# Two passes by halves in turn, six matmuls of zeros left out, and another order of sixteen chunks in a two-layer attention kernel

## The chip, the core and the metric

The kernel runs on one core of a Trainium2 chip. The metric is the device time in microseconds (us) of one execution. Engines are called as the profile calls them: PE (matmuls), PEld (PE's weight loads), ACT (activations), DVE (vector work), POOL, and SP, which here only issues DMAs; SPq, ACTq and POOLq are the queues of DMA issues.

## The reference, cut to what matters

```python
x = L0_attn_x                                   # (4, 1024, 128), 16 heads of 8
x = _layernorm(x + _L0_attn_ref(x, ...))        # q, k l2-normed over all 128 columns, softmax over 1024 keys
x = _layernorm(x + _L0_ffn_ref(x, ...))         # int8 quantized matmul
x = _layernorm(x + _L1_attn_ref(x, ...))        # layernorm and rope on q, k; causal softmax
x = _layernorm(x + _L1_ffn_ref(x, ...))         # silu(gate) * up, down; 384 hidden
```

Within an attention, for each batch, head and query:

```python
attn = softmax(q @ k.T * scale)                 # layer 1: keys up to the query alone
out = attn @ v
```

## The kernel before

**Chunks, passes, steps.** The 4 x 1024 rows are eight chunks of 512 rows, two to a batch. A layer's attention of one chunk is four *passes* of four heads each. A chunk is written (layer, number): (0, 2) is layer 0's attention for the queries of chunk 2, and needs the keys of chunks 2 and 3; (1, 3) needs the keys of chunks 2 and 3 too, and (1, 2) those of chunk 2 alone, since layer 1 is causal. `CHUNKS` (L48) is the order in which the sixteen pairs are worked through. `pair_steps` (L58) cuts two passes into *steps* of 128 keys by 512 queries for four heads (layer 1 packs parts of steps together). There are 400 steps: 32 in each chunk of layer 0, 10 or 26 in a chunk of layer 1. Step s has the score products k = 2s and 2s+1, two heads each.

**The three engines of a step.** PE makes the scores (`scores`, L964) in one of three slots of PSUM, ACT takes the exponential of each (L820, 800 in all), and PE multiplies the result with v (`sums`, L988). PE runs ahead of ACT: in *slot* s of its program it issues the scores 2s+3 and 2s+4, then the sums of step s-1, then at most one piece of *side work*. The scores of product k wait for exponential k-3. In layer 1 POOL sets the future part of the diagonal blocks to zero before the sums (L728).

**Side work.** All else is cut into pieces that a planner (`side_order`, L174) lays into the slots, by costs and due times: `prep` of a chunk (q, k, v of layer 0), `mid` (end of layer 0's block, its feed-forward part, and q, k, v of layer 1), `last` (end of layer 1's block and its feed-forward part). A job's pieces stay in order; a `mid` is due four slots ahead of the first slot of its chunk. The last two pieces of a `prep` or `mid` are called qkT: PE transposes k (k=1 in the code) and then q (k=0) of the chunk into PSUM, and DVE reads each into `part` as two summands (L1401, L1402). For the planner the qkT of `mid` 7 stand in slots 362 and 363; the first scores of (1, 7), which are product 748, stand in slot 372.

**The way of q and k.** From `part` SP stores them to DRAM, every row four times (`send_parts`, L548: two DMAs for k and two for q), and loads them back as the 128 rows that a pass needs, into `k_st` and `q_st` (`load_rows`, L572: one DMA each). Before a load SP waits until the stores of all chunks that the pass needs have landed, and until the pass four earlier has its scores. SP works through its DMAs in the order of the list `todo` (L634). The first scores of a pass wait for its rows (L969).

**The start.** `prep` of chunks 0 and 1 runs ahead of step 0. So as not to wait for DRAM, pass 0 gets its rows for chunk 0's keys straight from `part` by eight small DMAs (`first_rows`, half on SP, half on ACT), and those for chunk 1's keys by four more (L619), once chunk 1's k is transposed in slot 0; these keys are pass 0's steps 4 to 7. Pass 1's rows come from DRAM as all others do. Products of a tile of zeros (`warm`, `keep_warm`, L1032) stand in places of PE's program where it has nothing else to do, among them three in slot 0 and three in slot 1 (L1074).

Of the kernel before, what the change touches and what calls it, by code (L numbers as in the profile page):

```python
# [15 lines left out]
P = 128  # L16
# [28 lines left out]

CHUNKS = [(0, 0), (0, 1), (0, 2), (0, 3), (1, 0), (0, 4), (1, 1), (0, 5),  # L48
          (1, 2), (0, 6), (1, 3), (0, 7), (1, 4), (1, 5), (1, 6), (1, 7)]
PASSES = [(layer, c // NH2, c % NH2, g) for layer, c in CHUNKS for g in range(GB)]  # L50
NP = len(PASSES)

# [5 lines left out]
def pair_steps(p):  # L58

    layer, b, qh, g = PASSES[p]
    a, z = p, p + 1
    if not layer:
        kts = [[(x, kt)] for x in (a, z) for kt in range(KT)]
    elif qh:
        one = lambda x: [[(x, 0)], [(x, 1)], [(x, 5), (x, 7)], [(x, 2)], [(x, 4)], [(x, 3)]]
        kts = one(a) + [[(a, 6), (z, 6)]] + one(z)  # L70
    else:
        one = lambda x: [[(x, 0)], [(x, 1), (x, 3)]]
        kts = one(a) + [[(a, 2), (z, 2)]] + one(z)
    out = []
    for group in kts:
        tiles, at = [], 0
        for x, kt in group:
            lo = max(kt * P - qh * HALF, 0) if layer else 0
            tiles.append((x, kt, lo, at, HALF - lo))
            at += HALF - lo  # L80
        out.append((tuple(tiles), at, layer == 1 and group[0][1] * P >= qh * HALF))
    return out
# [305 lines left out]
def program(nc, a, ctx):  # L388
# [94 lines left out]
    x_first_in, x_rest_in, head_copied = sem("x_first_in"), sem("x_rest_in"), sem("head_copied")  # L483
    pool_consts, flags_made, late_consts = sem("pool_consts"), sem("flags_made"), sem("late_consts")
    rows_in = [sem(f"rows_in{n}") for n in range(KB)]
    more_rows_in = sem("more_rows_in")
    v_in, more_v_in = sem("v_in"), sem("more_v_in")
    scores_ready = sem("scores_ready")
    probs_ready = sem("probs_ready")
# [27 lines left out]
    shift_out, shift_in = sem("shift_out"), sem("shift_in")  # L517

    POOL_CONSTS = 11
    WARM = (10, 4, 0, 22, 3)  # L520
    NLATE = 9
    layer_job = ("prep", "mid")
    buffers = lambda name, c: job["mid" if (name, c) == ("prep", 1) else name]
# [9 lines left out]

        return b * NH2 + (NH2 if layer == 0 else qh + 1)

    def first_rows(eng, u, dst, y):

        part = job["prep"]["part"][0:P // PRODUCTS, u, y % PARTS if u else y // PARTS, :]
        eng.dma_start(dst[y:P:PRODUCTS, 0, 0:HALF].bitcast(F32), part.bitcast(F32)).then_inc(rows_in[0], 16)

    def parts_sent(eng, name, u, n):

        pools = (name, u) == ("prep", 1) and n > 1
        eng.wait_ge(parts_out[name][u], 16 * PARTS * (n - pools))
        if pools:
            eng.wait_ge(second_k_out, 16 * PARTS)
# [15 lines left out]
    def _(sp):  # L562
# [9 lines left out]
        def load_rows(p):  # L572
            layer, b, qh, g = PASSES[p]
            for u in range(2):
                parts_sent(sp, layer_job[layer], u, 1 if p == 1 and u == 0 else chunks_needed(layer, b, qh))
            if p >= KB:

                sp.wait_ge(scores_ready, 2 * (LAST_STEP[p - KB] + 1))
            keys = keys_of(layer, qh)
            rows(p, 1, k_st[:, p % KB, 0:keys], slice(0, keys), rows_in[p % KB])  # L580
            rows(p, 0, q_st[:, p % KB, :], slice(qh * HALF, (qh + 1) * HALF), rows_in[p % KB])

        def store_parts(name, c, u):
            send_parts(sp, name, c, u)
# [24 lines left out]
        for u, dst in ((1, k_st), (0, q_st)):  # L609
            sp.wait_ge(parts_ready["prep"], 2 - u)  # L610
            for y in range(PRODUCTS // 2):
                first_rows(sp, u, dst, y)
        store_parts("prep", 0, 1)
        store_parts("prep", 0, 0)
        sp.wait_ge(flags_made, 1)
        far_scores = sp.value_load(far_any[0:1, 0:1], min_val=0, max_val=1)
        sp.wait_ge(parts_ready["prep"], 3)
        for y in range(PRODUCTS):
            sp.dma_start(k_st[y:P:PRODUCTS, 0, HALF:S].bitcast(F32),  # L619
                         job["mid"]["part"][0:P // PRODUCTS, 1, y % PARTS, :].bitcast(F32)).then_inc(more_rows_in, 16)  # L620
        load_rows(1)
        store_parts("prep", 1, 0)

        def shift_rows(p):
# [150 lines left out]
    def _(act):  # L775
# [4 lines left out]
        def head():  # L780
# [25 lines left out]
            for u, dst in ((1, k_st), (0, q_st)):  # L806
                act.wait_ge(parts_ready["prep"], 2 - u)
                for y in range(PRODUCTS // 2, PRODUCTS):
                    first_rows(act, u, dst, y)

        head()

# [44 lines left out]
    def _(pe):  # L857
# [106 lines left out]
        def scores(k, shifted):  # L964

            s, tiles_ = k // 2, STEPS[k // 2][1]
            for p in dict.fromkeys(x[0] for x in tiles_):
                if k % 2 == 0 and FIRST[p] == s:
                    pe.wait_ge(rows_in[p % KB], 32 * (p // KB + 1) + (32 * PRODUCTS - 32 if p % KB == 0 else 0))  # L969
                    if shifted:  # L970
                        shifts(p)
            if k % 2 == 0 and tiles_[0][0:2] == (0, TC):
                pe.wait_ge(more_rows_in, 16 * PRODUCTS)
            if k >= SLOTS:

                pe.wait_ge(probs_ready, k - SLOTS + 1)
# [31 lines left out]
        def shifts(p):  # L1008
# [4 lines left out]
                pe.wait_ge(probs_ready, k)  # L1013
            if p == 0:
                pe.wait_ge(more_rows_in, 16 * PRODUCTS)
                pe.wait_ge(pool_consts, POOL_CONSTS + 1)
            for r in range(NR):
                h, t = divmod(r, TC)
# [38 lines left out]
        def steps(shifted):  # L1057
# [10 lines left out]
            for s in range(NS + 1):  # L1068
                for k in (2 * s + 3, 2 * s + 4):
                    if k < 2 * NS:  # L1070
                        scores(k, shifted)
                    if k % 2 and s in BETWEEN:
                        sums(s - 1)
                if s < 2 and not shifted:  # L1074
                    keep_warm(WARM[4], ACC)
                if s and s not in FRONT and s not in BETWEEN:
                    sums(s - 1)
                for name, c, e, what, k in SIDE_ORDER[s]:
# [14 lines left out]
    def _(dve):  # L1093
# [255 lines left out]
        def read(name, c, what, k):  # L1349
# [35 lines left out]
            elif what == "qkT":  # L1385
# [7 lines left out]
                    dve.wait_ge(more_rows_in, 16 * PRODUCTS)  # L1393
                if k == 1 and (name, c) == ("prep", 2):
                    dve.wait_ge(rows_in[0], 32 * PRODUCTS)
                if name == "prep" and k == 0:
                    ch.link(ts(part[:, 0, 0, :], side, tcol, None, ALU.mult))
                    stt(out=part[:, 0, 1, :], in0=side, scalar=tcol, in1=part[:, 0, 0, :].bitcast(F32), op0=ALU.mult,
# [135 lines left out]
```

## Time and profile before

| | |
|---|---|
| median of three runs | 834.07 us (833.52 to 834.15) |
| the profiled execution | 835.72 us, of it 833.6 us from the first to the last instruction (its span) |
| busy: PE, ACT, DVE, POOL | 804.5, 772.8, 540.5, 169.6 us |
| 800 exponentials on ACT | 749.8 us |
| mean granted TensorE clock | 0.991 of full speed |

The span is what the trace shows; the profiled execution's time is 2.1 us longer than its span. PE's busy time is modelled, so a share of 97% doesn't mean that it computes at its peak.

### The profile page before, as it was taken

The page shows a single profiled execution, that of the slowest core. Times are in us where ns is not written, and L with a number is a line of the kernel's source. Part 1 is how long each engine was busy: PE and PEld are TensorE (multiplying, and loading weights), DVE is VectorE, ACT ScalarE, POOL GpSimd, SP SyncE. Part 2 cuts the span into 40 slices and gives each one's busy share as a digit, 9 for nine tenths or more (in the row PEclk, how much of TensorE's full clock was granted, in tenths as well). Part 3 has the DMA queues.
Part 4 walks back from the last instruction along what each step waited for, and adds up shares of the span by engine and source line. Part 5 has one row for each costly group of instructions (what it writes and reads, how often), then busy time and mean ns, then how long its engine had stood idle before and what let it go on. Part 6 is the DMA issues. An engine that isn't in the chain of part 4 may idle for free.

```text
span 833.6 us, 18913 instructions
## 1 busy us (share of the span) xinstructions
PE 804.5 (97%) x7461; PEld 295.6 (35%) x7463; DVE 540.5 (65%) x1426; ACT 772.8 (93%) x869; POOL 169.6 (20%) x370
## 2 busy tenths in 40 slices
PE   8899999999999999999999999999999999999996
PEld 4223332332332433343333433343333343443444
DVE  4165657777867787877563577766664268786656
ACT  4699999999999999999999999999999999899972
POOL 3110000010000701033100521023300263363220
PEclk9799999999999999999999999999999999999999
DMA  5765412341611731173140331331231231062000
GB/s 163 257 195 190 172 45 103 125 141 52 245 47 49 268 135 43 62 247 99 39 152 27 116 103 50 127 103 39 77 127 52 77 116 51 27 202 90 15 14 15
DMA packets 48316, 88.74 MB, mean 106 GB/s; under 512 B 5088, under 2 KB 14432, under 8 KB 48224
## 3 DMA queue, kind: packets, MB, share of 16 engines
q1 hardware_dynamic: 47456, 85.95, 30.6%
q8 instruction: 61, 1.00, 0.5%
q0 software_dynamic: 288, 1.05, 0.4%
q10 hardware_dynamic: 480, 0.48, 0.2%
q14 instruction: 31, 0.25, 0.1%
HBM read 51.03 MB, written 35.65 MB: 104 GB/s over the span
## 4 chain that ended last, share of the span: by engine, by line
PE 75%; ACT 12%; DVE 7%; issue 3%; SPq 1%; DMA 1%; DVEq 0%; ACTq 0%
PE ps L1003 36%; PE ps L981 21%; ACT probs L820 12%; PE ps L873 9%; PE ps L862 3%; PE ps L958 3%; DVE th L1411 1%; DVE hT L1412 1%; DMA k_st<-mid_part 1%; PE ps L867 1%; PE ps L1034 1%; PE ps L1042 0%; SPq L554 0%; DVE sums_t L1240 0%; DVE mid_part L1401 0%
## 5 line engine op out<-in xcount | busy, mean ns | idle before, releaser
L820 ACT ACTIVATE probs<-ps 128x1024 f32<-128x1024 f32 x800 | 749.8, 1054 | 32.6 <-PE ps L981 23.2
L1003 PE MATMUL ps<-probs,v_st 128*32 128x512 f32 (+3 forms) x3584 | 428.5, 560 | 3.1 <-issue 2.4
L981 PE MATMUL ps<-q_st,k_st 32*128 32x512 f32 (+3 forms) x1792 | 266.2, 461 | 9.0 <-ACT probs L820 5.5
L981 PEld LDWEIGHTS ps<-q_st,k_st 32*128 32x128 f32 x1792 | 120.1, 182 | 290.0 <-ACT probs L820 223.6
L728 POOL TENSOR_SCALAR_AFFINE_SELECT probs<-probs 128x256 f32<-128x256 f32 x256 | 103.8, 428 | 143.3 <-ACT probs L820 141.6
L1003 PEld LDWEIGHTS ps<-probs,v_st 128*32 128x32 f32 x3584 | 78.6, 108 | 110.8 <-issue 74.2
L696 POOL COPY v_st<-v_all 128x256 f32<-128x256 f32 (+1 forms) x65 | 28.8, 452 | 365.7 <-PE ps L1003 357.3
L1240 DVE STREAM_TRANSPOSE sums_t<-ps 128x512 f32<-128x512 f32 x32 | 22.9, 716 | 45.2 <-PE ps L1003 44.6
L1381 DVE COPY mid_qkv<-ps 128x384 f32<-128x384 f32 x32 | 17.8, 558 | 35.9 <-PE ps L873 34.8
L958 PE MATMUL ps<-yTp,w_hid 128*128 128x512 f32 x84 | 30.8, 448 | 4.1 <-DVE gate_sb L1406 2.5
L1381 DVE COPY prep_qkv<-ps 128x384 f32<-128x384 f32 x24 | 13.4, 558 | 31.2 <-PE ps L873 30.5
L873 PE MATMUL ps<-w_cols,yT 128*32 128x384 f32 x256 | 26.7, 489 | 0.0
L1411 DVE SCALAR_TENSOR_TENSOR th<-th,gate_sb 128x512 f32<-128x512 f32 x21 | 14.9, 708 | 16.6 <-PE ps L958 16.2
L1416 DVE TENSOR_TENSOR last_y<-ps,last_y 128x128 f32<-128x128 f32 x24 | 7.0, 291 | 28.8 <-PE ps L873 28.4
L873 PE MATMUL ps<-w_down,hT 128*32 128x128 f32 x672 | 23.8, 275 | 1.1 <-DVE last_y L1416 0.6
L718 POOL TENSOR_TENSOR x_all<-x_all,vecs 128x512 f32<-128x512 f32 x16 | 23.3, 1458 | 0.0
L958 PEld LDWEIGHTS ps<-yTp,w_hid 128*128 128x128 f32 x84 | 12.5, 188 | 29.6 <-issue 9.4
L1358 DVE TENSOR_TENSOR x_all<-ps,x_all 128x512 f32<-128x512 f32 x15 | 10.4, 692 | 19.1 <-PE ps L873 11.5
L873 PEld LDWEIGHTS ps<-w_down,hT 128*32 128x32 f32 x672 | 17.9, 110 | 13.2 <-issue 7.5
L1406 DVE COPY gate_sb<-ps 128x512 f32<-128x512 f32 x21 | 14.5, 691 | 12.3 <-PE ps L958 12.0
L873 PE MATMUL ps<-w_cols,xT 128*32 128x384 f32 x192 | 20.1, 491 | 0.4 <-DVE hT L1412 0.2
L1401 DVE CAST mid_part<-ps 128x512 fp32r<-128x512 f32 x17 | 11.8, 692 | 11.9 <-PE ps L862 11.7
(190 smaller groups left out, 634.7 us busy)
## 6 DMA issues: line engine op xcount, KB each, us to landing
k_st<-parts_scratch SPq DMA_DIRECT2D x47, 512.0 KB, 3.6
parts_scratch<-mid_part SPq DMA_DIRECT2D x34, 512.0 KB, 4.3
q_st<-parts_scratch SPq DMA_DIRECT2D x63, 256.0 KB, 3.9
parts_scratch<-prep_part SPq DMA_DIRECT2D x28, 512.0 KB, 4.7
k_st<-parts_scratch SPq DMA_DIRECT2D x16, 256.0 KB, 2.9
xT<-in_xT SPq DMA_DIRECT2D x8, 256.0 KB, 4.3
x_all<-in_x SPq DMA_DIRECT2D x8, 256.0 KB, 5.5
out<-yo SPq DMA_DIRECT2D x7, 256.0 KB, 2.3
```

The source lines that it names most:

```text
L696: return g_.tensor_copy(v_st[:, p % VB, t, :, p % 2 * SR:p % 2 * SR + D], v_all[:, layer, b % 2, t, g * GH * D:(g + 1) * GH * D] .rearrang ...
L718: g_.tensor_tensor(x_all[:, c, :, :], x_all[:, c, :, :], bc(vecs[:, 3 * layer, :].unsqueeze(1), [P, TC, C]), ALU.add).then_inc(bias_added, 1)
L728: op = g_.affine_select(out=block_, in_=block_, compare_op=ALU.is_ge, fill=0.0, base=0, pattern=[[0, 2], [1, P]], channel_multiplier=-1)
L820: nc.scalar.activation(probs[:, k % PS, :, 0:w], slot(k)[:, :, 0:w], ACT.Exp).then_inc(probs_ready, 1)
L862: last_ = tp(dst[:, t * P:(t + 1) * P], src(t), idn[:])
L873: last_ = mm(dst[row, :], src[:, row], w, start=first, stop=last)
L958: last_ = mm(side, w_hid[:, 0 if what == "gate" else 1, k * P:(k + 1) * P], yTp[:, n, :], start=(n == 0), stop=(n == PARTS - 1))
L981: last_ = mm(slot(k)[:, e, at:at + n], k_st[row, p % KB, kt * P:(kt + 1) * P], q_st[row, p % KB, lo:HALF], start=True, stop=not shifted)
L1003: last_ = mm(acc[HR * h:HR * (h + 1), lo:HALF], v_st[:, p % VB, kt, h, :], probs[:, (2 * s + h // 2) % PS, h % 2, at:at + n], start=FIRST[ ...
L1240: v.transpose(sums_t[:], acc).then_inc(sums_turned, 1)
L1381: v.tensor_copy(job[name]["qkv"][:, k, :], side[:, 0:3 * C]).then_inc(side_read, 1)
L1411: chain[lane(name, c)].link(stt(out=th[:, k % 2, :], in0=th[:, k % 2, :], scalar=1.0, in1=gate_sb[:, k % 2, :], op0=ALU.add, op1=ALU.mult))
```

## The change

Three parts. The order of chunks: every chunk of layer 1 but the last two stands one place sooner; (1, 0) now follows (0, 2), where it followed (0, 3), and so on to (1, 5), which still follows (0, 7), while (1, 4) now stands ahead of (0, 7). The first two passes: their steps go pass 0 with chunk 0's keys, pass 1 with chunk 0's keys, pass 0 with chunk 1's keys, pass 1 with chunk 1's keys. For this pass 1's rows for chunk 0's keys are sent from `part` too, by eight DMAs on SP ahead of all stores, and the stores of chunk 0 stand behind the four DMAs of L619; pass 1's other keys come from DRAM by a load of their own with a semaphore of its own. The products of zeros in slots 0 and 1 are gone.

```diff
-CHUNKS = [(0, 0), (0, 1), (0, 2), (0, 3), (1, 0), (0, 4), (1, 1), (0, 5),
-          (1, 2), (0, 6), (1, 3), (0, 7), (1, 4), (1, 5), (1, 6), (1, 7)]
+CHUNKS = [(0, 0), (0, 1), (0, 2), (1, 0), (0, 3), (1, 1), (0, 4), (1, 2), (0, 5), (1, 3), (0, 6), (1, 4), (0, 7), (1, 5),
+          (1, 6), (1, 7)]
...
         kts = [[(x, kt)] for x in (a, z) for kt in range(KT)]
+        if not p:
+            kts = [[(x, kt)] for n in range(2) for x in (a, z) for kt in range(n * TC, (n + 1) * TC)]
...
-    WARM = (10, 4, 0, 22, 3)
+    WARM = (10, 4, 0, 22)
...
-    def first_rows(eng, u, dst, y):
-
-        part = job["prep"]["part"][0:P // PRODUCTS, u, y % PARTS if u else y // PARTS, :]
-        eng.dma_start(dst[y:P:PRODUCTS, 0, 0:HALF].bitcast(F32), part.bitcast(F32)).then_inc(rows_in[0], 16)
+    def first_rows(eng, p, u, dst, y):
+
+        part = job["prep"]["part"][p * HR:(p + 1) * HR, u, y % PARTS if u else y // PARTS, :]
+        eng.dma_start(dst[y:P:PRODUCTS, p, 0:HALF].bitcast(F32), part.bitcast(F32)).then_inc(rows_in[p], 16)
...
             for y in range(PRODUCTS // 2):
-                first_rows(sp, u, dst, y)
-        store_parts("prep", 0, 1)
-        store_parts("prep", 0, 0)
+                first_rows(sp, 0, u, dst, y)
+        for u, dst in ((1, k_st), (0, q_st)):
+            for y in range(PRODUCTS):
+                first_rows(sp, 1, u, dst, y)
...
-        load_rows(1)
+        store_parts("prep", 0, 1)
+        store_parts("prep", 0, 0)
+        parts_sent(sp, "prep", 1, 2)
+        rows(1, 1, k_st[:, 1, HALF:S], slice(HALF, S), second_rows_in)
         store_parts("prep", 1, 0)
...
-                    pe.wait_ge(rows_in[p % KB], 32 * (p // KB + 1) + (32 * PRODUCTS - 32 if p % KB == 0 else 0))
+                    pe.wait_ge(rows_in[p % KB], 32 * (p // KB + 1) + (32 * PRODUCTS - 32 if p % KB < 2 else 0))
...
+            if k % 2 == 0 and tiles_[0][0:2] == (1, TC):
+                pe.wait_ge(second_rows_in, 16)
...
-                if s < 2 and not shifted:
-                    keep_warm(WARM[4], ACC)
...
                 if k == 1 and (name, c) == ("prep", 2):
                     dve.wait_ge(rows_in[0], 32 * PRODUCTS)
+                    dve.wait_ge(rows_in[1], 32 * PRODUCTS)
```

**PE at the start.** These are PE's rows from the first scores (`ps<-q_st,k_st`) on; `mid_qk` holds chunk 1's k and q there, `warm` the zeros, and `probs,v_st` are sums. Before:

```order
L981 MATMUL ps<-q_st,k_st 128x512 x6
L862 MATMUL ps<-ident,mid_qk 128x128 x4
L981 MATMUL ps<-q_st,k_st 128x512 x4
L1034 MATMUL ps<-warm 128x512 x3
L981 MATMUL ps<-q_st,k_st 128x512 x4
L1034 MATMUL ps<-warm 128x512 x3
L1003 MATMUL ps<-probs,v_st 32x512 x4
L862 MATMUL ps<-ident,mid_qk 128x128 x4
```

Now:

```order
L989 MATMUL ps<-q_st,k_st 128x512 x6
L868 MATMUL ps<-ident,mid_qk 128x128 x4
L989 MATMUL ps<-q_st,k_st 128x512 x8
L1011 MATMUL ps<-probs,v_st 32x512 x4
L868 MATMUL ps<-ident,mid_qk 128x128 x4
```

The two groups of zeros are gone and nothing else moved there; from the ninth score product on the rows are pass 1's, where they were pass 0's second half of keys.

**SP at the start.** These are SP's DMAs from the first rows for pass 0 on (`k_st<-prep_part`) up to the stores of chunk 1's q (`parts_scratch<-mid_part`). Before:

```order
L539 DMA k_st<-prep_part 32x512 x2
L539 DMA q_st<-prep_part 32x512 x2
L554 DMA parts_scratch<-prep_part 256x1x512 x2
L554 DMA parts_scratch<-prep_part 128x2x512 x2
L616 TENSOR_LOAD far_any
L616 ISA x2
L619 DMA k_st<-mid_part 32x512 x4
L570 DMA k_st<-parts_scratch 128x1024
L570 DMA q_st<-parts_scratch 128x512
L554 DMA parts_scratch<-mid_part 128x2x512 x2
```

Now:

```order
L541 DMA k_st<-prep_part 32x512 x2
L541 DMA q_st<-prep_part 32x512 x2
L541 DMA k_st<-prep_part 32x512 x4
L541 DMA q_st<-prep_part 32x512 x4
L619 TENSOR_LOAD far_any
L619 ISA x2
L622 DMA k_st<-mid_part 32x512 x4
L556 DMA parts_scratch<-prep_part 256x1x512 x2
L556 DMA parts_scratch<-prep_part 128x2x512 x2
L572 DMA k_st<-parts_scratch 128x512
L556 DMA parts_scratch<-mid_part 128x2x512 x2
```

Eight small DMAs for pass 1 came in where the four stores of chunk 0 stood; the stores moved behind the four DMAs for chunk 1's keys, and pass 1's load from DRAM is k's second half alone.

**PE in the chunk (1, 6).** These are PE's rows in slots 366 to 369: the projection of the chunk before (`w_out,attn`), scores and sums of (1, 6), and the places where the two qkT of `mid` 7 (`ident,mid_qk`) may stand. Before:

```order
L873 MATMUL ps<-w_out,attn 32x128 x16
L981 MATMUL ps<-q_st,k_st 128x384 x2
L981 MATMUL ps<-q_st,k_st 128x128 x2
L981 MATMUL ps<-q_st,k_st 128x512 x2
L1003 MATMUL ps<-probs,v_st 32x256 x8
L981 MATMUL ps<-q_st,k_st 128x512 x2
L981 MATMUL ps<-q_st,k_st 128x384 x2
L981 MATMUL ps<-q_st,k_st 128x128 x2
L1003 MATMUL ps<-probs,v_st 32x512 x4
L981 MATMUL ps<-q_st,k_st 128x384 x2
```

Now:

```order
L879 MATMUL ps<-w_out,attn 32x128 x16
L989 MATMUL ps<-q_st,k_st 128x384 x2
L989 MATMUL ps<-q_st,k_st 128x128 x2
L989 MATMUL ps<-q_st,k_st 128x512 x2
L1011 MATMUL ps<-probs,v_st 32x256 x8
L868 MATMUL ps<-ident,mid_qk 128x128 x4
L989 MATMUL ps<-q_st,k_st 128x512 x2
L989 MATMUL ps<-q_st,k_st 128x384 x2
L989 MATMUL ps<-q_st,k_st 128x128 x2
L1011 MATMUL ps<-probs,v_st 32x512 x4
L868 MATMUL ps<-ident,mid_qk 128x128 x4
```

The two qkT of `mid` 7 now stand behind the projection, in slots 367 and 368; before they stood in slots 362 and 363, ahead of the first rows shown. The first scores of (1, 7) stand in slot 372 in both.

## Rows read from the trace of the kernel before

**Rows 1.** The page's busy time by engine, and its costliest group.

```profile
PE 804.5 (97%) x7461; PEld 295.6 (35%) x7463; DVE 540.5 (65%) x1426; ACT 772.8 (93%) x869; POOL 169.6 (20%) x370
...
L820 ACT ACTIVATE probs<-ps 128x1024 f32<-128x1024 f32 x800 | 749.8, 1054 | 32.6 <-PE ps L981 23.2
```

**Rows 2.** Timeline of ACT from 18 to 64 us: start, length, [idle before].

```profile
27.57 1.02 ACT L820 ACTIVATE probs<-ps 128x1024 f32<-128x1024 f32 x1 [0.61 <-PE ps L981]
31.90 1.94 ACT L820 ACTIVATE probs<-ps 128x1024 f32<-128x1024 f32 x2 [3.30 <-PE ps L981]
34.49 3.98 ACT L820 ACTIVATE probs<-ps 128x1024 f32<-128x1024 f32 x4 [0.66 <-PE ps L981]
40.09 24.70 ACT L820 ACTIVATE probs<-ps 128x1024 f32<-128x1024 f32 x26 [1.62 <-PE ps L981]
```

**Rows 3.** Timeline of PE from 22 to 34 us.

```profile
22.86 0.82 PE L1034 MATMUL ps<-warm 128*128 128x512 bf16 x3
...
27.46 1.06 PE L1003 MATMUL ps<-probs,v_st 128*32 128x512 f32 x8
31.00 0.80 PE L981 MATMUL ps<-q_st,k_st 32*128 32x512 f32 x4 [2.48 <-DMA k_st<-mid_part]
31.73 1.94 PE L1003 MATMUL ps<-probs,v_st 128*32 128x512 f32 x8
```

**Rows 4.** Busy time by stretch, all engines, with the granted clock (PEclk).

```profile
31.40:41.60 10.20, 10.20 (x52) 2.12 (x48) 0.00 (x0) 7.33 (x8) 0.00 (x0) 0.53 0.74 245
751.30:808.90 57.60, 55.10 (x658) 23.53 (x654) 33.90 (x98) 53.01 (x59) 15.76 (x38) 1.00 0.09 31
```

**Rows 5.** Timeline of SP's DMA issues from 14 to 42 us.

```profile
16.65 1.23 SPq L539 DMA_DIRECT2D q_st<-prep_part  x2
17.93 3.47 SPq L554 DMA_DIRECT2D parts_scratch<-prep_part  x4
22.92 4.21 SPq L619 DMA_DIRECT2D k_st<-mid_part  x4
```

**Rows 6.** DMA issues: KB each, median us from issue to landing.

```profile
q_st<-parts_scratch SPq DMA_DIRECT2D x63, 256.0 KB, 3.9
parts_scratch<-prep_part SPq DMA_DIRECT2D x28, 512.0 KB, 4.7
...
q_st<-prep_part SPq DMA_DIRECT2D x2, 64.0 KB, 2.1
```

**Rows 7.** Exponentials by stretch; a stretch is one chunk, first exponential to first exponential.

```profile
209.50:270.60 61.10, 59.60 (x65) 1.00 0.32 114
270.60:289.20 18.60, 18.38 (x21) 1.00 0.80 267
483.50:546.60 63.10, 60.07 (x65) 1.00 0.25 84
546.60:596.30 49.70, 48.45 (x53) 1.00 0.22 71
596.30:658.10 61.80, 59.74 (x65) 1.00 0.23 79
676.70:731.85 55.15, 49.61 (x53) 1.00 0.13 44
731.85:751.30 19.45, 18.56 (x21) 1.00 0.72 237
```

**Rows 8.** Timeline of all engines from 730 to 744 us.

```profile
730.63 1.31 DVE L1231 TENSOR_TENSOR mid_qk<-mid_qk,rot 128x1024 f32<-128x1024 f32 x1
...
732.14 0.63 PE L862 MATMUL ps<-ident,mid_qk 128*128 128x128 f32 x4 [0.29 <-DVEq L1232]
...
734.46 0.66 PE L862 MATMUL ps<-ident,mid_qk 128*128 128x128 f32 x4 [0.26 <-DVE mid_part L1402]
...
741.05 0.69 DVE L1358 TENSOR_TENSOR x_all<-ps,x_all 128x512 f32<-128x512 f32 x1 [0.59 <-PE ps L873]
...
743.92 0.43 SPq L570 DMA_DIRECT2D q_st<-parts_scratch  x1
```

More of the change, by code:

```diff
@@ L485, in program @@
     rows_in = [sem(f"rows_in{n}") for n in range(KB)]
-    more_rows_in = sem("more_rows_in")
+    more_rows_in, second_rows_in = sem("more_rows_in"), sem("second_rows_in")
     v_in, more_v_in = sem("v_in"), sem("more_v_in")
@@ L574, in load_rows @@
             for u in range(2):
-                parts_sent(sp, layer_job[layer], u, 1 if p == 1 and u == 0 else chunks_needed(layer, b, qh))
+                parts_sent(sp, layer_job[layer], u, chunks_needed(layer, b, qh))
             if p >= KB:
@@ L808, in head @@
                 for y in range(PRODUCTS // 2, PRODUCTS):
-                    first_rows(act, u, dst, y)
+                    first_rows(act, 0, u, dst, y)
         head()
@@ L1015, in shifts @@
                 pe.wait_ge(more_rows_in, 16 * PRODUCTS)
+            elif p == 1:
+                pe.wait_ge(second_rows_in, 16)
+            if p == 0:
                 pe.wait_ge(pool_consts, POOL_CONSTS + 1)
```

## The prediction

> **What bounds the kernel now.** I read the page's busy times first: ACT is busy 772.8 of 833.6 us, and 749.8 of that are the 800 exponentials [rows 1]. PE shows 97%, but that is modelled, so the question is where ACT stands still. Its timeline answers: at the start it waits four times, 0.61, 3.30, 0.66 and 1.62 us, 6.2 us in all; after that its exponentials follow each other at 24.70/26 = 0.95 us [rows 2]. PE's timeline says why: it waits 2.48 us for the DMAs of chunk 1's keys (L619), and from 31 us on each batch of sums takes 1.94 where it had taken 1.06 [rows 3], because the granted clock fell to half: 0.53 in the mean from 31.4 to 41.6 us, the 1.2 GHz level, after PE had stood idle [rows 4]. So 3.3 of the 6.2 us are the transfer and 2.3 (0.66 + 1.62) are the clock that fell for it. The rest of the time is read by chunk. A chunk of layer 0 with a feed-forward end (`last`) in its slots takes 63.1 or 61.8 us, one of layer 1 takes 18.6 or 49.7, and one stands out: (1, 5) with 55.15 [rows 7], in which the planner had to lay most of `mid` 7 and of `last` 4 side by side.
>
> **Halves in turn.** Pass 1's first half puts eight exponentials, 8 x 0.95 = 7.6 us, between pass 0's two halves. The keys that were waited for, there at 31.00 [rows 3], are then needed for the seventeenth exponential, at 28.6 + 7.6 = 36.2 us, and two exponentials earlier for PE, 34.3: covered by 3 us even if they come no sooner. What is late next? Pass 1's eight DMAs follow SP's first four at 1.23/2 = 0.62 us each from 17.93 [rows 5], so the last is issued at about 22.3 and lands 2.1 later [rows 6], at 24.4; PE wants it after the sums that end at 28.5 [rows 3]. Pass 1's second half waits for the stores, which now stand behind L619's DMAs: those are issued by 27.1, the four stores take 3.5 [rows 5], the last lands 4.7 later [rows 6], at 35.3, and the load at the price of a `q_st` load, 3.9, brings the keys at 39.3. They are needed eight exponentials after 34.3, at 41.9. That is the thinnest cover, 2.6 us. I count the waits of 3.30, 0.66 and 1.62 as gone and leave the 0.61, a wait for PE that two transposes and sums cause rather than a transfer: **-5.6 us**.
>
> **No products of zeros.** Each group of three took 0.82 us of PE [rows 3] in slots where ACT had its scores in time, so their own time is worth nothing (below nothing for no reason). What they may have paid for is the clock: without them PE only has score products between 21 and 25 us, each waiting for an exponential. If the clock falls there, it costs what it cost before, 2.3 us, and some 0.5 for the scores of the ninth exponential: +2.8 as the other end. I take 0, since the row shows a fall only after PE had had nothing at all to do for 2.5 us.
>
> **The order of chunks.** I compared the planner's lists of both orders, slot by slot. From (1, 2) to (1, 5) each chunk has now exactly the list that another chunk had: (0, 5) and (0, 7) that of the old (0, 6); (0, 6) that of the old (0, 7); (1, 2) and (1, 4) their own; (1, 3) and (1, 5) that of the old (1, 3). So their durations can be taken over: 63.1 twice, 61.8, 18.6 twice, 49.7 twice [rows 7]. (1, 0), (0, 3), (1, 1) and (0, 4) have new lists; by their load (three gates, about 16 us of side matmuls by the planner's own prices) I take 18.6, 63.1, 49.7 and 63.1. Sum: 3 x 18.6 + 4 x 63.1 + 61.8 + 3 x 49.7 = 519.1 us, against 731.85 - 209.5 = 522.35 before: **-3.2 us**, of which (1, 5) gives 5.4 and the others take some back. The new lists could be 1.5 us off either way.
>
> **The stall that the order makes.** `mid` 7 pays for this. It starts later against (1, 7), and its last piece, q's transposes, stands in slot 368 in place of 363, while the first scores of (1, 7) stay in slot 372. Behind those transposes hangs a chain: two reads by DVE, two stores of q behind two of k, SP's wait for their landing, two loads, PE's wait. Before, it ran from 734.46 to the issue of the load of q at 743.92 [rows 8], and that lands 3.9 later [rows 6], at 747.8: 13.4 us, and 0.5 for the scores (four took 0.80 at half the clock, [rows 3]). The first exponential of (1, 7) came at 751.3 [rows 7], so 3.0 us were to spare. Five slots are half of the ten steps of (1, 6), 19.45/2 = 9.7 us [rows 7]. 9.7 - 3.0 = 6.7 us are missing. A second count gives more: rope's last operation (1.31 us) now stands behind DVE's read of the projection, which ends at 741.74, so k's transposes can't start before 743.1; before they started at 732.14 [rows 8], and 732.14 + 9.7 is 741.8, 1.3 us less. That makes 8.0. I take **+7.4 us**, range 5.5 to 9.5. All that stands behind the waiting scores on PE waits too, and ACT, DVE and POOL with it; no other work is there to hide it.
>
> **The clock behind that stall.** PE then has nothing to do for longer than the 2.5 us after which the clock fell at the start. There the fall cost ACT 2.3 us [rows 2]; in (1, 7) PE is busy 55.1 of 57.6 us [rows 4], so it can make up less. Ends: 1.5 if the clock comes back sooner, 5.1 if half of 10.2 us is lost. I take **+3.0**, near the row. The Trainium skill ("TensorE: Matmul & The Clock Gate", HAM oscillation) describes the same thing, bursts of matmuls that start slow after each wait for a DMA, and its section on terms prices it as the throttled time times the share of the clock that is missing. By that rule the start's fall would have cost 5.1 and not 2.3, so here PE's reserve decides; the sum by the rule would be 837.8.
>
> **Sum.** -5.6 - 3.2 + 7.4 + 3.0 = +1.6 us. The profiled execution (835.72; span 833.6) is 1.65 above the median of 834.07; on the median the forecast is **835.7 us**, and a profile like that of before would show 837.3. A measurement of this kernel can't tell less than about 0.2%, 1.7 us, from no change; the forecast lies at that edge.
>
> **The rivals.**
> *The clock falls at the start too.* The +2.8 above: 838.5. For it: six products of zeros stood just there, and the stretch is the least busy one of PE. Against it: no wait for a DMA is left in it. The Trainium skill ("TensorE: Matmul & The Clock Gate", Part 1) speaks for it: the throttled clock is the default and activity releases it, so matmuls of zeros are activity that is taken away. No row shows this stretch without them.
> *The stall is small.* If the stores and loads run alone and land sooner, 4.5 us may be missing in place of 7.4, and with PE idle for less the clock may stay: 834.1 - 8.8 + 4.5 = 829.8, faster than before. It decides from a chain that is 3 us shorter than 13.4.
> *No stall.* If rows come in time after all, only the gains are left: 834.1 - 8.8 = 825.3. Against it: a store and a load take 4.7 and 3.9 us to land by their medians [rows 6], which alone is more than the four slots (7.8 us) between slots 368 and 372.
> *Halves without effect.* If pass 1's rows are late by as much as the old keys were, the 5.6 us stay: 841.3. Against it: the 3 us of cover above.
>
> **How the numbers follow.** Chances: the forecast 0.45 (its own range 833 to 838.5), the clock falling at both places 0.25, a small stall 0.18, no stall 0.07, halves without effect 0.05. The time is that of the first. The range of 829 to 840.5 leaves out no stall, most of the last, and the ends of the others, 2 in 10 together. Faster by over 0.2% (below 832.4): no stall and most of the small stall, 0.23. Slower (above 835.7): a little under half of the forecast's case, and nearly all of the second and last, 0.49. Within: 0.28.
>
> **What the profile would show.** Right: ACT's exponentials run on from 20.4 to over 60 us with no gap above 0.7, PE shows no wait for `k_st<-mid_part`, and the clock stays at full until near the end; (1, 5) takes about 49.7 us; ACT waits some 7 us before the first exponential of (1, 7), PE there for a DMA into `k_st` or `q_st`, and the granted clock is at half behind it. Wrong: a half clock between 21 and 40 us, a chunk (0, 3) or (0, 4) well over 64 us, or a gap ahead of (1, 7) under 4 us, which would make it faster.

## The result, and the profile after

The changed kernel takes **843.64 us** (median of four runs, 843.52 to 844.55), the kernel before in the same job 833.93: ratio 1.0122, interval 1.0101 to 1.0144. It is slower, the likeliest of the three outcomes (0.49), but by 9.7 us and not by 1.6, and the time lies above the range that was given. The profiled execution took 843.52 us, with a span of 841.4 (before: 833.6). The spans differ by 7.8 us and the medians by 9.7, since the profiled execution of before (835.72) was 1.8 us slower than its median. One thing is needed to read all that follows: executions of one and the same kernel differ in how long the clock is granted at half, so a single profile is one draw out of several.

The page of the changed kernel has the loss on ACT's line, and its cause on the line of PE's scores (both of the costliest groups; [rows 1] has the first of before):

```profile
L826 ACT ACTIVATE probs<-ps 128x1024 f32<-128x1024 f32 x800 | 750.2, 1053 | 40.4 <-PE ps L989 30.6
...
L989 PE MATMUL ps<-q_st,k_st 32*128 32x512 f32 (+3 forms) x1792 | 267.1, 460 | 16.3 <-DMA q_st<-parts_scratch 7.9
```

The exponentials take what they took (749.8, now 750.2), but ACT stands idle ahead of them for 40.4 us in place of 32.6, and 7.9 of PE's idle time are a wait for rows that come back from DRAM.

**The start.** ACT's timeline from 18 to 64 us, start, length and idle before ([rows 2]):

```profile
20.11 6.52 ACT L826 ACTIVATE probs<-ps 128x1024 f32<-128x1024 f32 x7 [4.07 <-PE ps L989]
28.41 1.02 ACT L826 ACTIVATE probs<-ps 128x1024 f32<-128x1024 f32 x1 [1.77 <-PE ps L989]
30.71 33.85 ACT L826 ACTIVATE probs<-ps 128x1024 f32<-128x1024 f32 x36 [1.28 <-PE ps L989]
```

The gap of 3.30 us is gone, and no wait for `k_st<-mid_part` is left. But the two gaps that remain, 1.77 and 1.28, go with a half clock, as PE's timeline of the same place shows (the same eight sums take 1.94 and 1.88 us and then 1.06):

```profile
22.10 0.50 PE L989 MATMUL ps<-q_st,k_st 32*128 32x512 f32 x2 [0.41 <-ACT probs L826]
...
24.66 1.94 PE L1011 MATMUL ps<-probs,v_st 128*32 128x512 f32 x8
...
28.29 1.88 PE L1011 MATMUL ps<-probs,v_st 128*32 128x512 f32 x8
...
30.54 1.06 PE L1011 MATMUL ps<-probs,v_st 128*32 128x512 f32 x8
```

This half clock begins at 23.1 us, where the products of zeros used to stand and where PE has only scores that each wait for an exponential. Windows of all engines (the stretch and its length; busy time of PE, PEld, DVE, ACT, POOL, each with its count; then the granted clock, the DMA share and GB/s) give its level, and that of the second one:

```profile
23.10:30.00 6.90, 6.67 (x26) 1.79 (x26) 1.59 (x3) 4.56 (x5) 2.51 (x7) 0.51 0.80 263
750.20:760.40 10.20, 4.31 (x30) 1.38 (x30) 1.02 (x4) 1.91 (x2) 0.84 (x3) 0.50 0.79 268
```

**By chunk.** Windows of the exponentials, one chunk each (the stretch, its length, the exponentials' busy time and count, the granted clock, the DMA share and GB/s; [rows 7]): (1, 0), (0, 3), (1, 1), (0, 4), (1, 5), (1, 6), (1, 7).

```profile
205.70:224.60 18.90, 18.46 (x21) 1.00 0.87 294
224.60:288.10 63.50, 60.28 (x65) 1.00 0.26 91
288.10:339.50 51.40, 49.05 (x53) 1.00 0.29 94
339.50:404.50 65.00, 60.34 (x65) 1.00 0.38 136
679.50:729.20 49.70, 48.43 (x54) 1.00 0.18 56
729.20:757.00 27.80, 18.99 (x22) 0.88 0.42 143
757.00:816.70 59.70, 50.27 (x52) 0.97 0.10 35
```

The fourth chunk begins at 205.7 where it began at 209.5: the start has given 3.8 us. From there to the end of (1, 5) it is 729.2 - 205.7 = 523.5 us, before 522.35: the middle gives nothing and costs 1.15. (1, 6) takes 27.8 for 19.45, +8.35, and (1, 7) 59.7 for 57.6 [rows 4], +2.1. Together +7.8, the difference of the spans. (1, 5) stands in the list where it stood; what became lighter is what is laid into its slots, 6.15 us of side matmuls by the planner's own prices where it was 15.95.

**The stall**, in the timeline of all engines from q's transposes to the first exponential of (1, 7) ([rows 8]):

```profile
742.15 0.66 PE L868 MATMUL ps<-ident,mid_qk 128*128 128x128 f32 x4
742.18 3.46 SPq L556 DMA_DIRECT2D parts_scratch<-mid_part  x4
751.20 0.33 SPq L572 DMA_DIRECT2D k_st<-parts_scratch  x1
751.57 0.43 SPq L572 DMA_DIRECT2D q_st<-parts_scratch  x1
...
756.09 0.80 PE L989 MATMUL ps<-q_st,k_st 32*128 32x512 f32 x2 [7.92 <-DMA q_st<-parts_scratch]
...
756.99 1.02 ACT L826 ACTIVATE probs<-ps 128x1024 f32<-128x1024 f32 x1 [7.18 <-PE ps L989]
```

From 742.15 to 756.09 are 13.9 us of transposes, reads, stores, landing, load, landing (13.4 had been counted), in which SP waits 5.6 us for the stores to land and PE stands still for 7.92.

### The profile page after: what moved, and what is told of

Read it like the earlier page. It is cut to its first block, busy times and chain, and to the rows that moved or that the text cites. A ratio compares the mean times of both kernels' runs of the same rounds, so it can differ in the third digit from the quotient of the medians.

```text
span 841.4 us, 18913 instructions
## 1 busy us (share of the span) xinstructions
PE 804.7 (96%) x7457; PEld 294.8 (35%) x7457; DVE 537.6 (64%) x1426; ACT 773.2 (92%) x869; POOL 173.4 (21%) x370
## 4 chain that ended last, share of the span: by engine, by line
PE 67%; ACT 18%; DVE 7%; issue 5%; DMA 2%; POOL 1%; ACTq 0%; SPq 0%; DVEq 0%; POOLq 0%
PE ps L1011 32%; PE ps L989 19%; ACT probs L826 17%; PE ps L879 8%; PE ps L868 3%; PE ps L964 3%; DMA parts_scratch<-mid_part 1%; DVE th L1421 1%; DVE hT L1422 1%; PE ps L873 1%; DMA q_st<-parts_scratch 1%; PE ps L1045 1%; DVE sums_t L1249 1%; DVE mid_part L1411 1%; DVE mid_part L1412 1%
## 5 line engine op out<-in xcount | busy, mean ns | idle before, releaser
L826 ACT ACTIVATE probs<-ps 128x1024 f32<-128x1024 f32 x800 | 750.2, 1053 | 40.4 <-PE ps L989 30.6
L734 POOL TENSOR_SCALAR_AFFINE_SELECT probs<-probs 128x256 f32<-128x256 f32 x256 | 106.8, 440 | 141.5 <-ACT probs L826 138.5
L1390 DVE COPY prep_qkv<-ps 128x384 f32<-128x384 f32 x24 | 13.4, 558 | 27.3 <-PE ps L879 26.7
L1421 DVE SCALAR_TENSOR_TENSOR th<-th,gate_sb 128x512 f32<-128x512 f32 x21 | 14.8, 704 | 14.3 <-PE ps L964 13.4
```

What stands on the lines that cost most here:

```text
L734: op = g_.affine_select(out=block_, in_=block_, compare_op=ALU.is_ge, fill=0.0, base=0, pattern=[[0, 2], [1, P]], channel_multiplier=-1)
L826: nc.scalar.activation(probs[:, k % PS, :, 0:w], slot(k)[:, :, 0:w], ACT.Exp).then_inc(probs_ready, 1)
L1390: v.tensor_copy(job[name]["qkv"][:, k, :], side[:, 0:3 * C]).then_inc(side_read, 1)
L1421: chain[lane(name, c)].link(stt(out=th[:, k % 2, :], in0=th[:, k % 2, :], scalar=1.0, in1=gate_sb[:, k % 2, :], op0=ALU.add, op1=ALU.mult))
```

## Experiments

All kernels compute everything. Times are medians; the ratio is that to the kernel before on the same chip (not the quotient of the two medians), and an effect in us that is taken from a ratio is its distance from 1 times 834. The medians of before differ between the jobs: 834.85 (e1 to e4), 832.72 (e5 to e8), 833.29 (e9, e10), 832.97 (e11, e12).

**Start alone (e1).** The changed kernel with `CHUNKS` as before.

```diff
-CHUNKS = [(0, 0), (0, 1), (0, 2), (1, 0), (0, 3), (1, 1), (0, 4), (1, 2), (0, 5), (1, 3), (0, 6), (1, 4), (0, 7), (1, 5),
-          (1, 6), (1, 7)]
+CHUNKS = [(0, 0), (0, 1), (0, 2), (0, 3), (1, 0), (0, 4), (1, 1), (0, 5),
+          (1, 2), (0, 6), (1, 3), (0, 7), (1, 4), (1, 5), (1, 6), (1, 7)]
```

> The halves in turn and no products of zeros, with the old order of chunks. Theory (the costs of the three parts add up, and the start still pays for a fallen clock): the start's trace as in the changed kernel, ACT's two gaps of about 1.8 and 1.3 us behind a granted clock at half, 3.9 us gained in all: about 830 us. Rival (the start gives nothing, its DMAs have moved the wait elsewhere): 834 us.

832.41 us, ratio 0.9977 (0.9961 to 0.9992): some -1.9 us. That is 2.4 us above the expected 830. In the profile the clock is at half for 3.4 us, from 24.3, where the changed kernel has 6.8; but the profiled execution is the fastest of the twelve (830.96, mean clock 0.996), and the other eleven have 0.990 to 0.993. All chunks from (0, 1) on are as before.

**Order alone (e2).** The kernel before with the new `CHUNKS`, the reverse of e1's edit.

> The new order of chunks with the old start. Theory: a gap of about 7 us on ACT ahead of (1, 7), a granted clock at half behind it, and (1, 1) and (0, 4) about 2 us longer each than the lists that I had taken for them: 845 to 847 us. Rival (the stall comes only with the new start, whose DMAs shift what SP does): under 837 us.

845.97 us, ratio 1.0145 (1.0112 to 1.0178): some +12.1 us, as expected. Middle and stall are those of the changed kernel (63.5, 51.4, 65.0; 27.6, 59.7). The two ratios multiply to 1.0122, the whole change. Its start has the code of before, and here is what one draw means (timeline of ACT, against [rows 2]):

```profile
27.65 1.02 ACT L820 ACTIVATE probs<-ps 128x1024 f32<-128x1024 f32 x1 [0.61 <-PE ps L981]
31.20 1.94 ACT L820 ACTIVATE probs<-ps 128x1024 f32<-128x1024 f32 x2 [2.53 <-PE ps L981]
33.80 31.11 ACT L820 ACTIVATE probs<-ps 128x1024 f32<-128x1024 f32 x33 [0.66 <-PE ps L981]
```

The gap of 1.62 us that counted in the sum is not there, since the half clock lasted 3.4 us and not 10.2: this execution spends 2.7 us less on (0, 0) (64.4 for 67.1).

**Zeros kept (e3).** e1 with the products of zeros in slots 0 and 1.

```diff
-    WARM = (10, 4, 0, 22)
+    WARM = (10, 4, 0, 22, 3)
...
+                if s < 2 and not shifted:
+                    keep_warm(WARM[4], ACC)
```

> As the first, but the products of zeros in slots 0 and 1 stay. Theory (the clock fell at the start for want of them): granted clock at full from 20 to 40 us, the gaps of 1.8 and 1.3 us shrink to under 1 us together, 2 to 2.5 us below the first, about 827.5 us. Rival (the gaps are PE's load at any clock, or the clock falls in any case): within 0.7 us of the first.

831.02 us, ratio 0.9958 (0.9942 to 0.9974). In the profiled execution the clock doesn't fall at all in the start (timeline of ACT):

```profile
27.30 1.02 ACT L826 ACTIVATE probs<-ps 128x1024 f32<-128x1024 f32 x1 [0.60 <-PE ps L989]
28.78 35.68 ACT L826 ACTIVATE probs<-ps 128x1024 f32<-128x1024 f32 x38 [0.46 <-PE ps L989]
```

(0, 0) takes 61.6 us, in e1 62.4, in the changed kernel 63.6. The zeros were worth 1.4 us by the medians, less than the 2 to 2.5 expected. The intervals of the two ratios overlap, but e1 and e3 ran in one job, and eleven of e1's twelve executions (831.75 us or more) are slower than the slowest of e3's (831.60).

**Five zeros (e9).** e3 with five products of zeros in place of three.

```diff
-    WARM = (10, 4, 0, 22, 3)
+    WARM = (10, 4, 0, 22, 5)
```

> The start by halves with the old order, as in the run with three products of zeros kept in slots 0 and 1, but five of them in each. In that run the executions fell into two groups, five at 829.5 to 829.9 us with a mean clock of 0.998 to 0.999 and seven at 830.9 to 831.6 with 0.995 or 0.996. Theory (a half clock in the start is what parts them, and too little work on PE there lets the clock fall): most executions belong to the first group, median 829.7, (0, 0) 61.6 us. Rival 1, the fall has to do with another place: two groups as before, about 831. Rival 2, four more products per slot pair delay the scores: (0, 0) over 62.5, 832 or more.

830.53 us, ratio 0.9963 (0.9945 to 0.9981). Eight of twelve executions now lie at 829.96 to 830.54, seven of them with a mean clock of 0.998 or 0.999 (in e3 five of twelve), but the profiled one has the clock at half from 21.2 to 24.6 all the same: more zeros make a fall rarer at best, and they don't exclude it.

**The old wait filled (e10).** The kernel before, with ten products of zeros ahead of the wait for chunk 1's keys.

```diff
             if k % 2 == 0 and tiles_[0][0:2] == (0, TC):
+                if not shifted:
+                    pe.wait_ge(probs_ready, k - SLOTS + 1)
+                    for _ in range(FILL_WAIT):
+                        mm(slot(k)[:, 0, :], warm[:, 0:P], warm[:], start=True, stop=True)
                 pe.wait_ge(more_rows_in, 16 * PRODUCTS)
```

> The kernel before, with ten products of zeros on PE ahead of the wait for chunk 1's keys (into the bank of the score slot that is free by then). The wait itself stays. Theory (of the gain of the halves some 2.5 to 3.3 us are the transfer and about 2 the clock that falls behind the wait): the granted clock stays whole from 30 to 41 us, ACT's gap of 2.5 to 3.3 us stays, the gaps of 0.66 and 1.62 go, (0, 0) takes 64 to 65 us in place of 67.1; the median is 1 to 2 us below before, ratio 0.998 to 0.999. Rival, the fall is not made by that wait: the clock falls all the same and the ratio is 1.000.

833.39 us, ratio 0.9998 (0.9983 to 1.0013). The profile does as expected (timeline of ACT):

```profile
31.22 32.95 ACT L821 ACTIVATE probs<-ps 128x1024 f32<-128x1024 f32 x35 [2.80 <-PE ps L986]
```

In the start the clock stays whole, the gap of the transfer stays, the two of the clock are gone, (0, 0) takes 63.9. The median doesn't fall by the 1 to 2 us expected. Two readings are left. One is that in many executions of before that clock is not there to be won, as e2 shows for one. The other is that the clock falls elsewhere instead: in this profile it is at half for 3.4 us in (1, 5) (a window of all engines), which takes 56.15 us there for 55.07 in the profile of before:

```profile
706.20:709.60 3.40, 3.40 (x17) 0.70 (x20) 2.84 (x6) 1.54 (x3) 0.11 (x1) 0.50 0.00 0
```

How much each of the two has in it is not shown. For (0, 0) the three profiles of the old start part the terms: 63.9 with no half clock, 64.4 with 3.4 us of it (e2), 67.1 with 10.2. So the long half clock cost some 3.2 us there and the short one some 0.5. Against e3 the transfer alone is 63.9 - 61.6 = 2.3 us, not 3.3.

**The stall filled (e4).** The changed kernel with 30 products of zeros on PE ahead of the wait for (1, 7)'s rows.

```diff
+            if not shifted and k == 2 * FIRST[NP - GB]:
+                pe.wait_ge(probs_ready, k - SLOTS + 1)
+                for _ in range(FILL_WAIT):
+                    mm(slot(k)[:, 0, :], warm[:, 0:P], warm[:], start=True, stop=True)
```

> The changed kernel with thirty products of zeros on PE, about 6.5 us of work, between the last scores of (1, 6) and the wait for the rows of (1, 7). Theory (the clock falls because PE stands idle there, and that costs some 2 us beside the stall itself): ACT's gap of about 7 us stays, the granted clock stays at full, (1, 7) takes 57.5 in place of 59.7 us, 841 to 842 us. Rival (the clock is of no account there, (1, 7) is longer for other reasons): 843 to 844 us.

841.20 us, ratio 1.0085 (1.0061 to 1.0110). PE's timeline: the wait is filled, and the sums behind it take 1.07 at once.

```profile
747.69 6.42 PE L977 MATMUL ps<-warm 128*128 128x512 bf16 x29 [0.16 <-issue]
755.38 0.50 PE L994 MATMUL ps<-q_st,k_st 32*128 32x512 f32 x2 [1.26 <-DMA q_st<-parts_scratch]
755.80 1.07 PE L1016 MATMUL ps<-probs,v_st 128*32 128x256 f32 x16
```

The clock stays whole, ACT still waits 6.81 us, and (1, 7) takes 58.0 for 59.7: the half clock costs 1.7 us there, and (1.0122 - 1.0085) x 834 = 3.1 by the ratios, whose intervals overlap a little. It is not one draw: all six executions have a mean clock of 0.991 to 0.995, the changed kernel's four 0.988 or 0.989.

**Early half of the order (e5).** e3's start; the new order, but (1, 4) stays behind (0, 7).

```diff
-CHUNKS = [(0, 0), (0, 1), (0, 2), (1, 0), (0, 3), (1, 1), (0, 4), (1, 2), (0, 5), (1, 3), (0, 6), (1, 4), (0, 7), (1, 5),
-          (1, 6), (1, 7)]
+CHUNKS = [(0, 0), (0, 1), (0, 2), (1, 0), (0, 3), (1, 1), (0, 4), (1, 2), (0, 5), (1, 3), (0, 6), (0, 7),
+          (1, 4), (1, 5), (1, 6), (1, 7)]
```

> The start of the changed kernel with the three products of zeros kept in slots 0 and 1, and the new order of chunks except that (1, 4) stays behind (0, 7). Theory (the planner's list of a chunk sets its duration, and the stall is mid 7 coming too late against (1, 7)): mid 7's qkT stand in slots 362 and 363 again, so (1, 6) and (1, 7) take 19.4 and 57.5 us as before and PE keeps its clock; (1, 0), (0, 3), (1, 1), (0, 4) take 18.9, 63.5, 51.4 and 65.0 as in the changed kernel, (0, 7), now without a last, 60.8 to 61.8, and (1, 5) 55.1. That is 4.5 us more than the old order with the same start (831.0): about 835.5, ratio 1.001. Rival 1, the four long chunks are long for another reason than their lists: about 831. Rival 2, the stall does not hang on where mid 7 stands: 845 or more.

834.43 us, ratio 1.0010 (0.9995 to 1.0026): the time is as expected. No stall; (0, 4), (1, 5) and (1, 6) in windows of the exponentials:

```profile
337.90:402.80 64.90, 60.28 (x65) 1.00 0.38 136
...
674.50:729.60 55.10, 49.58 (x54) 1.00 0.12 44
729.60:749.00 19.40, 18.51 (x21) 1.00 0.73 243
```

The new lists cost 0.5% against e3 by the ratios. Between the two profiles, from the fourth chunk to the start of (1, 6), it is 525.6 for 522.4 us, +3.2 where 4.5 were counted ((0, 7) takes 59.8 only); and the clock, which was to stay whole, fell in (1, 7), which takes 59.0 for 57.5. So two errors partly cancel in the time.

**Late half of the order (e6).** e3's start; the old order up to (1, 2), then the new one.

```diff
-CHUNKS = [(0, 0), (0, 1), (0, 2), (0, 3), (1, 0), (0, 4), (1, 1), (0, 5),
-          (1, 2), (0, 6), (1, 3), (0, 7), (1, 4), (1, 5), (1, 6), (1, 7)]
+CHUNKS = [(0, 0), (0, 1), (0, 2), (0, 3), (1, 0), (0, 4), (1, 1), (0, 5), (1, 2), (1, 3), (0, 6), (1, 4),
+          (0, 7), (1, 5), (1, 6), (1, 7)]
```

> The same start with zeros kept, the old order up to (0, 5) and (1, 2), then (1, 3), (0, 6), (1, 4), (0, 7), (1, 5) as in the new order: only the late half is moved. Theory: (0, 3), (1, 0), (0, 4) and (1, 1) take 61.1, 18.6, 64.1 and 49.8 as before, (1, 3) some 51 and (0, 6) some 64 by new lists, (0, 7) 63.1, (1, 5) 49.7, and the stall is whole: (1, 6) 27.8, (1, 7) 59.7. Against the old order with this start (831.0) that is -2.0 in the middle and +10.5 at the end: about 839.5, ratio 1.006. Rival, the stall needs the early half of the order too (mid 7 late because all is late): (1, 6) stays at 19.4 and the time is about 829.

839.02 us, ratio 1.0077 (1.0057 to 1.0097): as expected. (0, 3) and (0, 4) are as before, (1, 5) is the short one, the stall is whole:

```profile
203.80:264.90 61.10, 59.59 (x65) 1.00 0.32 114
283.60:347.70 64.10, 60.64 (x65) 1.00 0.24 84
...
674.70:724.40 49.70, 48.43 (x53) 1.00 0.17 56
724.40:752.20 27.80, 19.01 (x21) 0.87 0.43 144
```

**Rows of (1, 7) without DRAM (e7).** e3's start, the whole new order; pass 60 gets q and its newest keys straight from `part`.

```diff
+        def last_rows(u):
+
+            p, c = NP - GB, NCH - 1
+            dst = (q_st, k_st)[u]
...
+            for y in range(PRODUCTS):
+                sp.dma_start(dst[y:P:PRODUCTS, p % KB, HALF if u else 0:S if u else HALF].bitcast(F32),
+                             job["mid"]["part"][0:HR, u, y % PARTS if u else y // PARTS, :].bitcast(F32)).then_inc(rows_in[p % KB], 16)
...
+                elif (what, n) == ("mid", NCH - 1):
+                    last_rows(u)
+                    if u == 0:
+                        store_parts(what, n, 1)
+                        store_parts(what, n, 0)
```

> The whole new order and the start with zeros kept; pass 60, the first of (1, 7), gets q and its keys of chunk 7 straight from part by eight small DMAs, and its keys of chunk 6 by a load of their own, with the stores of mid 7 behind them. Theory (the stall is the trip through DRAM, store, landing, load, landing): first rows land by about 750, the gap of 7.2 us ahead of (1, 7) falls to under 1 us, (1, 6) takes 19.5 to 20.5, the clock stays whole and (1, 7) takes 57.5 to 59 (pass 61's rows come some 5 us later than in the changed kernel and may cost up to 1 us). Against the old order with this start (831.0): +1.1 for the middle, 0 to 2 for the end: 832 to 834, ratio 0.998 to 1.000. Rival, PE waits there for the transposes and the projection ahead of them rather than for DRAM: a gap of 4 us or more stays, 838 or more.

834.73 us, ratio 1.0008 (0.9990 to 1.0025), just above the expected 832 to 834. ACT's timeline ahead of (1, 7):

```profile
750.20 1.03 ACT L845 ACTIVATE probs<-ps 128x1024 f32<-128x1024 f32 x1 [0.56 <-PE ps L1008]
751.57 1.94 ACT L845 ACTIVATE probs<-ps 128x1024 f32<-128x1024 f32 x2 [0.34 <-PE ps L1008]
755.11 1.94 ACT L845 ACTIVATE probs<-ps 128x1024 f32<-128x1024 f32 x2 [1.60 <-PE ps L1008]
```

The gap of 7.18 us is 0.56: the stall is the trip through DRAM. The end is dearer than expected, (1, 6) with 21.2 and (1, 7) with 59.5, where the clock fell for 3.4 us from 751.4 (the profiled execution is the slowest of the twelve, 836.59). Of the 8.35 us by which (1, 6) is longer in the changed kernel, the gap ahead of (1, 7) is 7.18; the other 1.2 lie inside (1, 6), and they are still there in e7, where the two qkT stand in the same slots. PE, too, still waits 1.60 us ahead of the first scores of (1, 7).

**Late half without DRAM (e8).** e6 with the edit of e7.

> The late half of the new order alone (as the run before last) with the direct rows for pass 60 (as the run before). Theory: the gain of (1, 5) is kept, neither the early lists nor the stall are paid: -2.0 us against the old order with this start, +0 to 2 at the end, so 829 to 831, ratio 0.993 to 0.996. Rival, what (1, 5) gives is taken back by the new lists of (1, 3) and (0, 6): 833 or more.

832.05 us, ratio 0.9993 (0.9977 to 1.0008), a miss by 1 to 3 us: (1, 3) 51.0 and (0, 6) 64.0 are as counted, but (1, 6) and (1, 7) take 21.3 and 59.5 here too, 3.9 us together in place of 0 to 2. Against the old order with this start (e3, 0.9958) that is no gain.

**One transposition sooner (e11).** The changed kernel, in slot 164 (of (0, 4)) DVE's transposition of the heads right behind the sums' turn.

```diff
 SIDE_ORDER, JOBS, FRONT, BETWEEN = side_order()
+SIDE_ORDER[164].sort(key=lambda x: x[3] not in ("turn", "yT"))
```

> The changed kernel, with one move in DVE's order: in slot 164, the first of (0, 4), the transposition of the heads that the projection waits for stands right behind the sums' turn, where the read of chunk 7's first qkv and five operations of mid 3 (rs1) stood between. Theory (the new list of (0, 4) is dear because these stand ahead of the projection, which holds PE and the next scores): PE's wait of 0.80 us for attn goes, ACT's gap of 1.15 us there falls under 0.3, and (0, 4) takes 63.8 to 64.2 us in place of 65.0; nothing else moves. Rival, the projection itself makes the gap: (0, 4) stays at 65.0. The whole time moves by about 1 us, which this one look is not for.

One run, 841.77 us. In the changed kernel that place reads so (timeline; the five `mid_st` operations run from 345.36 to 346.85):

```profile
344.88 0.56 DVE L1390 COPY prep_qkv<-ps 128x384 f32<-128x384 f32 x1
345.36 0.22 DVE L1217 TENSOR_SCALAR mid_st<-mid_st 128x128 f32<-128x128 f32 x1
...
346.85 0.71 DVE L1256 STREAM_TRANSPOSE attn<-heads_t 128x512 f32<-128x512 f32 x1
347.70 1.08 PE L879 MATMUL ps<-w_out,attn 128*32 128x128 f32 x32 [0.80 <-DVE attn L1256]
...
349.25 1.03 ACT L826 ACTIVATE probs<-ps 128x1024 f32<-128x1024 f32 x1 [1.15 <-PE ps L989]
```

and in e11:

```profile
343.83 0.71 DVE L1257 STREAM_TRANSPOSE attn<-heads_t 128x512 f32<-128x512 f32 x1
344.46 0.52 DVE L1391 COPY prep_qkv<-ps 128x384 f32<-128x384 f32 x1
...
345.66 1.06 PE L880 MATMUL ps<-w_out,attn 128*32 128x128 f32 x32
```

PE's wait and ACT's gap are gone, and (0, 4) takes 64.0 us: 1.0 of its surplus of 1.9 was this one place.

**All transpositions sooner (e12).** e3 with that sort in every slot.

```diff
+for items in SIDE_ORDER:
+    items.sort(key=lambda x: x[3] not in ("turn", "yT"))
```

> The best start (halves in turn, three products of zeros kept) with the old order, and the same move in all five slots where another operation of DVE or a read of PE's result stands between turn and transposition. Theory: 0.2 to 1.0 us less in each place where the projection was held (slots 138, 170 and 338 of it), 829.5 to 831 us, ratio 0.994 to 0.996; rival, the pieces that step back hold their own followers: 831 or more.

832.34 us, ratio 0.9987 (0.9971 to 1.0003): a miss. No chunk between (0, 1) and (1, 6) is shorter than in e3 by more than 0.1 us; in the old order nothing waited at these places. The profiled execution had the clock at half for 3.4 us in the start and for 3.4 us in (1, 7).

## Why the prediction was wrong

The direction and the stall were right; two terms of the sum, those with a gain in them, were mis-sized, by 3.7 and 4.4 us, which is the whole miss of 8.1. The other two terms are off by +0.95 and -0.9, which cancel. Two of the prediction's own signs of being wrong showed: a half clock between 21 and 40 us, and (0, 4) at 65.0.

**Halves in turn and no zeros: -5.6 and 0 were counted, -1.9 is measured (e1).** By the ratios of e3 and e1 that parts into -3.5 for the halves with the zeros kept and +1.6 for leaving them out. The mechanism of the halves holds: the wait for chunk 1's keys is gone, the covers sufficed, no new wait for a DMA came, and "Halves without effect" is refuted. Two sizes were off.

The first is that the gain was read off one execution with a long half clock. For that execution it is right: (0, 0) takes 67.1 us there and 61.6 in e3, 5.5 less, though it parts otherwise than was read, 2.3 for the transfer and 3.2 for the clock in place of 3.3 and 2.3 (e10). But by their mean clock most executions of before don't have it whole. Of 29 in one job, 22 with a mean clock of 0.994 to 0.997 took 831.07 to 833.99 us, and seven with 0.990 or 0.991 took 835.63 to 836.72; the profiled one (835.72, 0.991) is of the second kind. In the other three jobs 13 of 23, 7 of 23 and 7 of 17 have 0.991 or less. The mean clock tells how much of an execution was at half, not where; that it was the start is seen in two profiles alone (10.2 us in that of before, 3.4 in e2).

The second is that "I take 0" for the zeros failed: the rival "The clock falls at the start too" came true in its mechanism (+2.8 was its price, +1.6 is measured), in the changed kernel from 23.1 us on, 3.6 us after PE's last wait for a DMA (0.61 us). The argument was that the row shows a fall only after PE had had nothing to do for 2.5 us; one row showed that such a wait can come ahead of a fall, not that it is needed.

**The order of chunks: -3.2 was counted, +1.15 is measured.** All durations that were taken over from matching lists held to 0.1 us (63.1 twice, 61.9, 18.6 twice, 49.7 twice). The four with new lists were sized "by their load" and are 0.3, 0.4, 1.7 and 1.9 us dearer, where 1.5 either way had been allowed for their sum. Load alone doesn't set it: (0, 4) and (0, 5) carry the same load by the planner's prices (15.75 and 15.95 us of side matmuls) and take 65.0 and 63.1. Which piece stands ahead of which matters too, as e11 shows for 1.0 us. For (1, 1) not even the load matched: it carries 11.0 us of side matmuls by these prices, and (1, 3), whose 49.7 was taken for it, 6.15. What makes up the rest of (0, 4) and the surplus of (1, 1) was not tried. e5 shows the lists' cost apart from the stall.

**The stall: +7.4 was counted, +8.35 is measured.** Its place, its chain (13.4 counted, 13.9 found) and its price are right, inside the range of 5.5 to 9.5; the gap itself is 7.18, and the other 1.2 lie inside (1, 6) (e7). e6 shows that it needs only the late half of the order, e5 that it goes when (1, 4) stays behind (0, 7), e7 that it goes when the rows skip DRAM. "The stall is small" and "No stall" are refuted.

**The clock behind it: +3.0 was counted, 2.1 is measured,** 1.7 to 3.1 by e4. The fall itself is right, but the size was taken from the start for a reason that doesn't hold here. At the start PE was busy in all of the 10.2 us that [rows 4] shows. Around the stall it was busy in 4.31 of the 10.2 us at half, because the clock fell at 750.2 us, while PE stood waiting until 756.09: half of 4.31 is 2.2, by estimate all that could be lost, and 2.1 is what was lost. That the term came out near is in part luck. By the rule of the Trainium skill ("TensorE: Matmul & The Clock Gate", HAM oscillation), the throttled time times the missing share, the estimate for these 10.2 us is 5.1. The trace doesn't agree; it is more than twice the 2.1 measured.

**The sum and the median.** That a profile 1.65 us above its median can simply be shifted to it was the hidden step: the stretch from which the first term was read had the longer half clock in it, and so a surplus that most executions don't have was counted as a gain of the median.

## What to carry to other kernels

Before a gain is read off one profile, see whether the stretch would look the same in another execution of the same kernel; a mean clock beside each run's time tells whether it is a usual one, though not where the clock fell. When an order of work is moved, count for the last consumer how many steps are left between its last producer and itself, and lay the whole chain (transposes, reads, stores, landing, load, landing) against them: here 13.9 us against four steps. Durations could be taken over here where the list of pieces was the same, to 0.1 us; where it was new, taking them from a similar load was up to 1.9 us off.

The version that does best here is the start by halves with the zeros kept and the old order: 0.9958 (e3), 0.9963 with five zeros (e9), 0.9987 with an order on DVE that changes nothing (e12, whose interval takes in 1), so some 0.1 to 0.4% below the kernel before.

## What was not expected of the hardware

The same code met half clocks of different length. In the old start it lasted 10.2 us in one profile (before) and 3.4 in another (e2). In the start by halves it lasted 6.8 us (the changed kernel, e4, e11) or 3.4 (e1) without the zeros, and with them 3.4 (e5, e6, e7, e9, e12) or nothing (e3, e8): in these profiles the zeros shorten it and don't rule it out. It also fell for 3.4 us far from any wait of PE for a DMA: in e9 at 703.8 us and in e10 at 706.2, both in (1, 5), and in e5 at 755.8 us, in (1, 7). PE had just waited 1.22, 1.22 and 1.30 us there, for DVE's copy into `gate_sb`; (1, 5) took 56.1 us in e9 and e10 for 55.1. In the profiles of before, e1 and e3 PE waits as long at both places, and the clock stays whole. Why the same place sometimes keeps its clock stays open.
